# Layer 1's experts: VectorE makes the high parts of three of the four hidden pairs in the blocks after an expert's first

## The reference

```python
gate_logits = x @ gate_w + gate_b
topk_vals, topk_idx = jax.lax.top_k(gate_logits, K)          # K = 2 of E = 8
comb = jnp.sum(one_hot(topk_idx) * softmax(topk_vals)[..., None], axis=2)
h = jax.nn.gelu(jnp.einsum('btd,edf->ebtf', x, w1) + b1[:, None, None, :], approximate=False)
y = jnp.einsum('ebtf,efd->ebtd', h, w2) + b2[:, None, None, :]
output = jnp.einsum('ebtd,bte->btd', y, comb)
```

## Time and profile before

| what | value |
|---|---|
| median of 3 runs | 1602.8 us (1600.75 to 1604.12) |
| profiled execution | 1604.2 us, its span 1602.3 us |
| TensorE matmul busy | 1392.9 us, 87% of the span |
| VectorE busy | 834.8 us, 52% |
| ScalarE busy | 713.1 us, 45% |
| GpSimd busy | 552.5 us, 34% |
| mean granted TensorE clock | 0.932 of full speed |

### The profile page before, as it was taken

One profiled execution on the slowest core, in us unless ns is written; L12 is line 12 of the kernel. 1 busy time (PEld: TensorE's weight loads), 2 busy tenths in 40 slices (PEclk: granted clock), 3 DMA queues, 4 the chain that ended last, 5 costly groups with the idle time before them and its releaser, 6 DMA issues. The chain is left out here.

```text
span 1602.3 us, 25436 instructions
## 1 busy us (share of the span) xinstructions
PE 1392.9 (87%) x9908; PEld 1288.8 (80%) x9908; DVE 834.8 (52%) x1654; ACT 713.1 (45%) x1375; POOL 552.5 (34%) x389
## 2 busy tenths in 40 slices
PE   5899989899867999999989995999889678987996
PEld 5776858768647899899889995988888668987996
DVE  3655656655664446446435223556666865455421
ACT  3354444444343454444444443454343425443553
POOL 1200001001025466566565441122120266566543
PEclk8899999999987999999999997998989769998998
DMA  3302031110115343443442223021202165444222
GB/s 128 120 24 67 27 95 43 52 61 27 66 51 156 94 86 81 116 106 92 105 104 47 47 42 100 24 88 41 72 30 80 54 193 119 102 106 109 48 42 35
DMA packets 72147, 123.30 MB, mean 77 GB/s; under 512 B 7440, under 2 KB 53152, under 8 KB 71968
## 3 DMA queue, kind: packets, MB, share of 16 engines
q1 hardware_dynamic: 46816, 81.92, 15.6%
q0 software_dynamic: 25152, 39.01, 13.4%
HBM read 96.12 MB, written 24.79 MB: 75 GB/s over the span
## 5 line engine op out<-in xcount | busy, mean ns | idle before, releaser
L2324 DVE TENSOR_TENSOR m_hidden_lo<-m_act_out,m_hidden_hi 128x512 fp32r<-128x512 f32 x224 | 162.6, 727 | 393.9 <-ACT m_hidden_hi L2267 368.5
L395 PE MATMUL banks<-m_down_hi,m_hidden_hi 128*128 128x256 f32 x896 | 267.9, 299 | 17.5 <-DVE m_hidden_lo L2324 11.3
L395 PE MATMUL banks<-m_down_hi,m_hidden_lo 128*128 128x256 f32 x896 | 263.7, 294 | 1.5 <-issue 1.5
L395 PE MATMUL banks<-m_down_lo,m_hidden_hi 128*128 128x256 f32 x896 | 263.9, 295 | 0.3 <-issue 0.3
L395 PEld LDWEIGHTS banks<-m_down_hi,m_hidden_hi 128*128 128x128 f32 x896 | 181.6, 203 | 22.2 <-issue 20.4
L395 PE MATMUL banks<-m_xt_hi,m_up_hi 128*128 128x256 f32 x640 | 186.6, 291 | 6.4 <-issue 6.4
L395 PE MATMUL banks<-m_xt_lo,m_up_hi 128*128 128x256 f32 x640 | 183.2, 286 | 0.0
L395 PE MATMUL banks<-m_xt_hi,m_up_lo 128*128 128x256 f32 x640 | 183.1, 286 | 0.0
L395 PEld LDWEIGHTS banks<-m_down_hi,m_hidden_lo 128*128 128x128 f32 x896 | 181.1, 202 | 1.7 <-issue 1.7
L395 PEld LDWEIGHTS banks<-m_down_lo,m_hidden_hi 128*128 128x128 f32 x896 | 181.5, 203 | 0.6 <-issue 0.6
L2401 POOL DMA_INDIRECT m_other_block<-rows,list_i x116 | 120.8, 1042 | 148.5 <-DVE list_i L1453 100.6
(11 more groups left out here) (367 smaller groups left out, 3555.0 us busy)
## 6 DMA issues: line engine op xcount, KB each, us to landing
stage<-in_down SPq DMA_DIRECT2D x22, 512.0 KB
stage<-in_ctx_cols SPq DMA_DIRECT2D x26, 402.0 KB
stage<-in_ctx_rows SPq DMA_DIRECT2D x20, 512.0 KB
stage<-in_up SPq DMA_DIRECT2D x20, 512.0 KB
m_stage<-in_up SPq DMA_DIRECT2D x11, 512.0 KB
m_stage<-in_down SPq DMA_DIRECT2D x10, 512.0 KB
rows<-xn SPq DMA_DIRECT2D x8, 528.0 KB, 3.7
stage<-in_ctx_picked SPq DMA_DIRECT2D x8, 512.0 KB
```

What stands on the lines that cost most here:

```text
L395: mm = q.e.matmul(dst, a, b, start=first and n == 0, stop=last and n == 2, skip_group_check=True)
L2324: q.e.tensor_tensor(lo, m.act[(n * HP + h) % ACTS], f32(hi), ALU.subtract).then_inc(*hidden_lo.mark((layer, n, h)))
```

## The change

In layer 1, in blocks with j > 0, and for the pairs h = 1, 2 and 3, ScalarE makes only the two gelus. VectorE waits for them and for the down products of the block before, makes the high part itself by a cast into `hi`, waits for its own cast by a new semaphore `hidden_hi_here`, and subtracts. For the last pair (h = 3) it does so in two tiles of 128x256, each after its own gelu. The first pair, all first blocks and layer 0 keep ScalarE's copy. In `scalar_pair` the wait for `up_done` now stands behind the one for `hidden_lo` in the source; this holds for all blocks of both layers. The new semaphore is one more in VectorE's catch-up.

```diff
+        hidden_hi_here = signal("hidden_hi_here")
...
+        def high_on_vector(layer, j, h):
+
+            return layer == 1 and j > 0 and h > 0
+
+        def by_tile(layer, j, h):
+
+            return layer == 1 and j > 0 and h == HP - 1
+
...
         def scalar_pair(q, layer, e, j, h):
             m, n = exp[layer], numbered(e, j)
             a = m.act[(n * HP + h) % ACTS]
-            q.wait_ge(*up_done.of(layer, n, h))
             q.wait_ge(*hidden_lo.of(layer, *earlier_use(n, h, ACTS)))
             src = up_ring.of((layer, n, h))
+            q.wait_ge(*up_done.of(layer, n, h))
             if layer == 0:
                 q.e.activation(a, src, gelu[0]).then_inc(*activated.mark((layer, n, h)))
             else:
                 for f in range(2):
                     c = slice(f * BLOCK, (f + 1) * BLOCK)
                     q.e.activation(a[:, c], src[:, c], gelu[1], bias=col("b1", e * HT + 2 * h + f)).then_inc(
-                        *activated.mark((layer, n, h)))
+                        *activated.mark((layer, n, h, f)))
+                activated.at[layer, n, h] = activated.count
+            if high_on_vector(layer, j, h):
+                return
             q.wait_ge(*activated.last())
             q.wait_ge(*down_done.of(layer, n - 1, h))
             q.e.activation(m.hidden[h][0], a, ACT.Copy).then_inc(*hidden_hi.mark((layer, n, h)))
...
         def vector_low(q, layer, e, j, h):
             m, n = exp[layer], numbered(e, j)
             hi, lo = m.hidden[h]
-            q.wait_ge(*hidden_hi.of(layer, n, h))
-            q.e.tensor_tensor(lo, m.act[(n * HP + h) % ACTS], f32(hi), ALU.subtract).then_inc(*hidden_lo.mark((layer, n, h)))
+            a = m.act[(n * HP + h) % ACTS]
+            if not high_on_vector(layer, j, h):
+                q.wait_ge(*hidden_hi.of(layer, n, h))
+                q.e.tensor_tensor(lo, a, f32(hi), ALU.subtract).then_inc(*hidden_lo.mark((layer, n, h)))
+                return
+            q.wait_ge(*down_done.of(layer, n - 1, h))
+            tiles = [slice(f * BLOCK, (f + 1) * BLOCK) for f in range(2)] if by_tile(layer, j, h) else [slice(0, 2 * BLOCK)]
+            for f, c in enumerate(tiles):
+                q.wait_ge(*activated.of(layer, n, h, f if len(tiles) > 1 else 1))
+                q.e.tensor_copy(hi[:, c], a[:, c]).then_inc(*hidden_hi_here.mark())
+                q.wait_ge(*hidden_hi_here.last())
+                q.e.tensor_tensor(lo[:, c], a[:, c], f32(hi[:, c]), ALU.subtract).then_inc(*hidden_lo.mark((layer, n, h)))
...
-            b, own = BATCH - 1, [block_lo, hidden_lo, handed]
+            b, own = BATCH - 1, [block_lo, hidden_lo, hidden_hi_here, handed]
```

## The result

After the change the kernel takes 1614.15 us (median of 9 runs, 1608.36 to 1621.82), before it 1604.12 us (9 runs, 1597.78 to 1610.95): ratio 1.0063, interval 1.0040 to 1.0086. I had forecast 1601.8 us, 1596.0 to 1606.5, and gave "slower" 0.19. The profiled execution took 1614.15 us with a span of 1612.3, against 1602.3 before.

What follows compares the result with a forecast made beforehand. TensorE was taken as the bound, fed without pause inside experts and waiting at their ends. Terms -0.8 - 0.4 - 0.6 + 0.8 = -1.0 us took 1604.2 to 1603.2; the median, 1.4 lower, gave 1601.8 us, range 1596.0 to 1606.5.

Steps and rivals of the forecast that it cites:

- Short ends: Four waits of TensorE, about 2.42 us each, at ends of layer 1's experts: 0.2 us less each, -0.8 us.
- The floor of 0.78: At expert ends, jump and catch-up need 0.78 us from VectorE's last issue until TensorE goes on.
- Long ends: Three longer TensorE waits at layer 1's expert ends: two gain 0.2 us each (-0.4), one gains 0.6.
- the third: Long end of 4.13 us in layer 1, let go by ScalarE's catch-up: -0.6 us (0 to -1.0).
- Rival 1: ScalarE's late third pair at layer 1's long ends disappears: 5.7 us less, 1596; chance 0.20.
- The untouched single-block end: TensorE's 5.93 us wait ending a layer 1 expert with only its first block: untouched, so no gain counted.
- rival 3: VectorE's longer program in j > 0 blocks gets a late place of its own: +7 us, 1608.8; chance 0.10.
- Swapped waits: ScalarE's separate late wait costs 0.05 us at sixteen expert ends of both layers: +0.8 us (0 to +1.8).
- The clock: TensorE's low-clock stretches behind expert ends, 1.5 to 3 us each: taken as unchanged, a term of nothing.
- Rival 4: VectorE's new casts are held up by GpSimd's DMA issues at the ends: +5.1 us, 1607.9; chance 0.08.

Runs made afterwards that it cites:

- swap_l0: Kernel before with ScalarE's two waits of a pair swapped in layer 0 only; 1604.59 us, ratio 1.0015.
- late4: Kernel before plus four empty ScalarE instructions before the last pair's gelu, which were not in the compiled program; 1606.43 us, ratio 0.9994.
- swap_only: Kernel before with only ScalarE's two waits of each pair swapped, in both layers; 1612.01 us, ratio 1.0041.
- no_swap: Changed kernel with ScalarE's two waits put back in their old order; 1606.41 us, ratio 1.0004 to the kernel before.
- whole: Changed kernel with the old order of waits and the last pair in one piece of 128x512; 1602.55 us, ratio 0.9986 to the kernel before.
- longer: Kernel before with eight empty VectorE instructions in each j > 0 block of layer 1; 1610.97 us, ratio 1.0043.
- tiles_short: Changed kernel with the old order of waits and VectorE's new work in blocks 1 to 4 only; 1610.38 us, ratio 1.0019 to the kernel before.
- late: Kernel before plus four empty ScalarE instructions, each with a semaphore increment, before the last pair's gelu in both layers; 1608.62 us, ratio 1.0041.
- fill5: Kernel before plus five TensorE transposes of the identity where it has left an expert's blocks, ahead of its catch-up; 1613.18 us, ratio 1.0036.

## Why the prediction was wrong

The step that failed is the price of the swapped waits. I had put it at +0.8 us (0 to +1.8), the sum of the delays at the ends, and the clock at nothing. The runs show 6.6 us (3.5 to 9.8) for the swap alone, most of it as time at 1.2 GHz. Why the clock falls more often stays open. Term by term:

- **Short ends, -0.8.** Failed. The four came from 9.71 to 9.77 us. The floor of 0.78 was right, but I started the tiles at the gelus' end and not behind VectorE's own queue, which then has cast and subtraction of the pair before. The swap's 0.06 is in it too. And I counted layer 1's first end among the four, though TensorE's own queue lets it go; it reads 2.45 before and 2.12 in swap_l0, with the same code there.
- **Long ends, -1.0 with the third.** The sum went from 13.83 to 12.25 us, -1.6, the forecast sign. That is luck as far as the runs show: late4, the same program as before, has 12.75 there, and swap_l0, the same code in layer 1, has 7.8. At the earlier trace rows ScalarE's catch-up starts 1.8 us after its branch, in late4 1.0. So the working step by step was finer than the rows allowed. ScalarE's late pair comes and goes in the same expert from kernel to kernel; Rival 1 did not happen in the changed one.
- **The untouched single-block end, 0.** Failed, +2.4. I had left it out as one that the change doesn't touch. This is rival 3's mechanism, a price for a longer VectorE program, at a jump and not inside a block.
- **Swapped waits, +0.8.** The delay was right (0.05 assumed, 0.06 measured, at fourteen ends and not sixteen), and the term wrong by a factor of eight (four to twelve). Two comparisons say so: swap_only's 1.0041, and 1.0063 - 1.0004 = 0.0059 ± 0.0030 between the change and no_swap.
- **The clock, set to nothing.** This is how most of the loss shows; it is not a further cost beside the swap's. The changed kernel spends 12 to 19 us more at 1.2 GHz, worth 6 to 9 us of the 10.0. My price of 1.5 to 3 us for a lost stretch fits the example: with 14 matmuls for 25, 1.3 us are lost in its three microseconds alone. But I only asked how often one of layer 1's seven ends would change side. In the trace the time that came on top lies ahead of layer 1's experts, in part where no instruction was changed.
- **Rival 4** (casts blocked by GpSimd's DMA issues) did not happen. In the timeline after, GpSimd's issue runs from 1548.42 to 1549.54, and the second tile's cast starts inside it at 1548.61 and takes 0.29. The slowest of the 48 new casts, one of 128x512 beside such an issue, took 0.62, just over the 0.6 that I had named as the sign; in whole one took 0.67. None waited for the whole issue. By the rule of the Trainium skill (SBUF — State Buffer, Who interferes with whom) the one that comes second would be blocked until the first has finished; these casts were not.

What stays open: why swap_only, longer, tiles_short and the change spend 8 to 19 us more at 1.2 GHz, while late, with longer waits, does not, and none of the swap's parts does. In the first three the difference is 2.6 to 4.8 times its standard error, and late4 shows -0.7 for an equal program. I could not reduce it to one wait. That it belongs to the timing of the whole program is a guess; a rival that no run tests is where the instructions come to lie in memory.

## What to carry to other kernels

Where TensorE's clock falls behind some waits and not behind equal ones, a small edit can cost several times its own delay (here 6.6 us for under 1), and a longer delay need not. So compare the granted clock over many runs before believing or undoing a small edit, take a second trace of the same program before placing a loss in one, and test the incidental edit (here two swapped lines) apart from the intended one. Count the length of a program with branches as a resource: instructions that never run lengthened a wait. And when work is moved to an engine, start its chain where that engine's queue is free, not where its input is ready.

## What the runs showed of the hardware

- A jump over blocks is not free for anyone. At the single-block end 0.78 us pass from VectorE's last issue to the released engine, and 3.2 once its program has 3634 instead of 3522 instructions. The step lies between VectorE's branch and its next instruction, 0.5 and 2.9 us. On TensorE 1.1 to 2.2 us pass before the first transpose behind the jump (fill5). VectorE's branches themselves take 43 to 67 ns in the trace before. The Trainium skill (Advanced Engine Details and Errata, Control Flow Timing) gives a compare-and-branch about 108 ns. By either figure the branch is a small part of these times.
- Four empty instructions with a signal between ScalarE's wait and its gelu cost 0.31 us (late), one separate wait 0.06 (swap_only).
- The same code of layer 1 waits 29.5 us at its eight ends in one program (before), 28.3 in another execution of it (late4) and 23.1 in a program that differs in layer 0 alone (swap_l0).
- Equal waits, 2.18 us, at the same place of the same program: the clock stays at 2.4 GHz in one execution and falls to 1.2 in the other.
